# Row maxima and exponentials taken over two PSUM banks at a time

## The reference, cut to what matters

```python
xn = _layernorm(x)
q, k, v = (xn @ Wq, xn @ Wk, xn @ Wv)            # 16, 4 and 4 heads of 16, then rotary angles on q and k
scores = einsum('bshd,bthd->bhst', q, k) / 4
out = einsum('bhst,bthd->bshd', softmax(scores), v) @ Wo
g = silu(ffn(xn))                                 # silu(gate) * up, then down; inner width 1024
x = x + out * g
...                                               # second block: linear attention, 8 routed experts
```

## Time and profile before

| what | us |
|---|---|
| three runs | 353.35, 356.22, 357.67 |
| their median | 356.22 |
| the profiled execution | 353.23 |
| its span, first to last instruction | 351.2 |

### The profile page before, as it was taken

The page is one execution under the profiler, slowest core; times in us unless marked ns, Lnnn a source line. Parts: engine busy times, 40 slices in busy tenths (PEclk is TensorE's granted clock), DMA queues, the critical chain, the costliest instruction groups (busy, mean ns, idle before and its releaser), DMA issues.

```text
span 351.2 us, 4689 instructions
## 1 busy us (share of the span) xinstructions
PE 319.4 (91%) x1598; PEld 188.7 (54%) x1598; DVE 230.7 (66%) x489; ACT 155.8 (44%) x282; POOL 67.4 (19%) x72
## 2 busy tenths in 40 slices
PE   3977799999999999999999999998986999999960
PEld 3655565445555544555554555465654566666640
DVE  3997849767575677877957711289995754456631
ACT  1477414676667455553674564411204222323220
POOL 4008650000020000000000000020673000346641
PEclk9999989999999999999999999998998999999997
DMA  7980000000000000000000040059226990424510
GB/s 245 411 218 2 0 1 2 0 4 0 1 3 2 1 0 3 0 0 4 1 2 1 0 167 15 0 216 367 77 97 189 400 424 32 154 89 136 154 51 11
DMA packets 11370, 30.56 MB, mean 87 GB/s; under 512 B 1773, under 2 KB 8014, under 8 KB 10064
## 3 DMA queue, kind: packets, MB, share of 16 engines
q1 hardware_dynamic: 9392, 26.01, 20.4%
q0 software_dynamic: 1952, 4.22, 3.9%
HBM read 27.22 MB, written 6.60 MB: 96 GB/s over the span
## 4 chain that ended last, share of the span: by engine, by line
PE 74%; DVE 14%; issue 3%; DMA 3%; POOL 2%; ACT 2%; DVEq 0%; POOLq 0%
PE ps L1578 11%; PE ps L1523 9%; PE ps L1491 8%; PE ps L1591 8%; PE ps L1513 7%; PE ps L1646 6%; PE ps L1632 5%; PE ps L1654 5%; PE ps L1428 3%; DVE nmax L1103 3%; PE ps L1453 2%; POOL slot_rows L787 2%; PE ps L1407 2%; PE ps L1622 1%; DMA x<-in_x 1%
## 5 line engine op out<-in xcount | busy, mean ns | idle before, releaser
L1103 DVE TENSOR_REDUCE nmax<-ps 128x1 f32<-128x512 f32 x128 | 85.5, 687 | 34.5 <-PE ps L1491 33.8
L907 ACT ACTIVATE shared<-ps 128x512 f32<-128x512 f32 x128 | 74.2, 594 | 53.8 <-PE ps L1513 52.7
L1491 PE MATMUL ps<-experts 96*128 96x512 bf16 x128 | 48.2, 384 | 1.6 <-DVE experts L1110 1.1
L1513 PE MATMUL ps<-experts 99*128 99x512 bf16 x128 | 48.5, 382 | 0.0
L1591 PE MATMUL ps<-shared,experts 128*128 128x256 f32 x128 | 38.0, 386 | 0.0
L1523 PE MATMUL ps<-shared,experts 128*32 128x512 f32 x256 | 34.1, 605 | 0.3 <-ACT shared L907 0.3
L1491 PEld LDWEIGHTS ps<-experts 96*128 96x128 bf16 x128 | 12.5, 98 | 36.7 <-DVE nmax L1103 18.3
L1591 PEld LDWEIGHTS ps<-shared,experts 128*128 128x128 f32 x128 | 23.3, 191 | 9.8 <-issue 3.4
L777 POOL TENSOR_TENSOR experts<-experts,late_weights 128x768 f32<-128x768 f32 x1 | 1.8, 1805 | 130.8 <-ACT experts L897 130.8
L1428 PE MATMUL ps<-late_weights,xnT 128*128 128x512 f32 (+1 forms) x64 | 23.9, 522 | 0.5 <-DVE shared L1069 0.5
L915 ACT ACTIVATE experts<-ps 96x1024 bf16<-96x1024 bf16 x18 | 17.9, 1018 | 11.6 <-PE ps L1453 11.6
(11 more groups left out here) (209 smaller groups left out, 526.9 us busy)
## 6 DMA issues: line engine op xcount, KB each, us to landing
experts<-in_experts SPq DMA_DIRECT2D x8, 1536.0 KB, 12.6
shared<-in_wgu SPq DMA_DIRECT2D x1, 2048.0 KB, 11.1
slot_rows<-in_empty SPq DMA_DIRECT2D x1, 1950.0 KB, 19.5
late_weights<-slot_rows SPq DMA_DIRECT2D x9, 130.0 KB, 4.2
x<-in_x SPq DMA_DIRECT2D x2, 512.0 KB, 5.5
shared<-in_wdn SPq DMA_DIRECT2D x1, 1024.0 KB, 13.1
token_rows<-x SPq DMA_DIRECT2D x1, 1024.0 KB, 14.4
token_rows<-gx SPq DMA_DIRECT2D x1, 1024.0 KB, 4.9
```

The lines of the kernel that those rows point to most:

```text
L907: nc.scalar.activation(probs[:, n % 2, hh, :], ps[:, 2 + hh % 2, :], ACT.Exp, scale=float(HD) ** -0.5).then_inc(s["exp_done"], 1)
L1103: nc.vector.tensor_reduce(nmax[:, 4 * t + hh:4 * t + hh + 1], ps[:, m % 2, :], AX, ALU.max, negate=True).then_inc(s["max_done"], 1)
L1491: nc.tensor.matmul(ps[:, m % 2, :], qs[0:KS, b, GR * g + hh, P * t:P * t + P], ks[0:KS, b, g, :], start=True, stop=True).then_inc(s["score ...
L1513: nc.tensor.matmul(ps[:, 2 + hh % 2, :], ks[0:KM, b, g, P * t:P * t + P], qs[0:KM, b, GR * g + hh, :], start=True, stop=True).then_inc(s[" ...
```

## The change

A score item becomes a pair of heads: two matmuls into banks 0 and 1, one reduction over both banks that writes two columns of `nmax`. A prob item likewise: two matmuls into banks 2 and 3, one exponential over both. There are then 64 of each where there were 128. Both banks of a pair are read by one instruction, so score pair `m` waits for maximum `m - 1`, and prob pair `q` for exponential `q - 1`. In the loop, a step's first and third place take a prob pair with a score pair right behind it; where a unit's last scores fall due, and in step 0, further score pairs stand at the second (and fourth) place. The values item comes after the score pairs of its place, no longer before them. The planner's assumed durations become 0.44 for a pair on TensorE, 1.1 for an exponential and 1.2 for a maximum. The written-out start keeps its seven transposes and six filling items, now between eight pairs. The count of matmuls stays the same, and every other item is as before.

```diff
-SCORES_OF = ((0, 4), (4, 9), (9, 13), (13, 16))
+SCORES_OF = ((0, 2), (2, 4), (4, 6), (6, 8))
+PAIRS_U = GR * TB // 2
...
-    PE = {"prob": .22, "score": .22, "values": .9, "stack_T": .45, "gate": .65, "up": .65, "down": .43, "heads_norm": .43, "max_rows": .22,
+    PE = {"prob": .44, "score": .44, "values": .9, "stack_T": .45, "gate": .65, "up": .65, "down": .43, "heads_norm": .43, "max_rows": .22,
...
-            self.other("act", .48, ("exp", GR * item[1] + item[2]), t)
+            self.other("act", 1.1, ("exp", 2 * item[1] + item[2]), t)
         elif kind == "score":
-            self.other("dve", .6, ("max", item[1]), t)
+            self.other("dve", 1.2, ("max", item[1]), t)
...
-    for m in range(16):
+    between = ("tt", "t", "te", "tt", "et", "ee", "e", "e")
+    queue = stacks[3:]
+    for m, kinds in enumerate(between):
         plan.append(("score", m))
-        if m in (0, 1, 3, 4, 6, 7, 9):
-            plan.append(stacks[3 + (0, 1, 3, 4, 6, 7, 9).index(m)])
-        elif m in (5, 8, 10, 11, 12, 14):
-            if emit() == ("hidden", 0):
+        for kind in kinds:
+            if kind == "t":
+                plan.append(queue.pop(0))
+            elif emit() == ("hidden", 0):
                 later.append(plan.pop())
...
-            items = [("prob", n, hh)]
+            items = [("prob", n, hh // 2)] if hh % 2 == 0 else []
+            cut = int(bool(scores) and (n == 0 or hh % 2 == 0 or t == TB - 2))
+            items += scores[:cut]
+            scores = scores[cut:]
             if hh == 1 and n > 0:
                 items.append(("values", n - 1))
-            cut = -(-len(scores) // (GR - hh))
-            items += scores[:cut]
-            scores = scores[cut:]
...
-                    nc.scalar.activation(probs[:, n % 2, hh, :], ps[:, 2 + hh % 2, :], ACT.Exp,
+                    nc.scalar.activation(probs[:, n % 2, 2 * hp:2 * hp + 2, :], ps[:, 2:4, :], ACT.Exp,
                                          scale=float(HD) ** -0.5).then_inc(s["exp_done"], 1)
...
-                    nc.vector.tensor_reduce(nmax[:, 4 * t + hh:4 * t + hh + 1], ps[:, m % 2, :], AX, ALU.max,
+                    nc.vector.tensor_reduce(nmax[:, GR * t + 2 * hp:GR * t + 2 * hp + 2].rearrange("p (a o) -> p a o", o=1), ps[:, 0:2, :], AX, ALU.max,
                                             negate=True).then_inc(s["max_done"], 1)
...
-                    if m >= 2:
-                        pe.wait_ge(s["max_done"], m - 1)
-                    nc.tensor.matmul(ps[:, m % 2, :], qs[0:KS, b, GR * g + hh, P * t:P * t + P], ks[0:KS, b, g, :],
-                                     start=True, stop=True).then_inc(s["score_ready"], 1)
+                    if m:
+                        pe.wait_ge(s["max_done"], m)
+                    for a in range(2):
+                        last = nc.tensor.matmul(ps[:, a, :], qs[0:KS, b, GR * g + 2 * hp + a, P * t:P * t + P], ks[0:KS, b, g, :],
+                                                start=True, stop=True)
+                    last.then_inc(s["score_ready"], 1)
...
-                    if q >= 2:
-                        pe.wait_ge(s["exp_done"], q - 1)
-                    nc.tensor.matmul(ps[:, 2 + hh % 2, :], ks[0:KM, b, g, P * t:P * t + P], qs[0:KM, b, GR * g + hh, :],
-                                     start=True, stop=True).then_inc(s["prob_ready"], 1)
+                    if q:
+                        pe.wait_ge(s["exp_done"], q)
+                    for a in range(2):
+                        last = nc.tensor.matmul(ps[:, 2 + a, :], ks[0:KM, b, g, P * t:P * t + P], qs[0:KM, b, GR * g + 2 * hp + a, :],
+                                                start=True, stop=True)
+                    last.then_inc(s["prob_ready"], 1)
```

More of the change, by code:

```diff
@@ L137, in needs @@
         if kind == "prob":
-            _, n, hh = item
-            out = [("exp", GR * n + hh - 2)]
-            return out + [("moved", n // TB)] if hh == 0 and n % TB == 0 else out
+            _, n, hp = item
+            out = [("exp", 2 * n + hp - 1)]
+            return out + [("moved", n // TB)] if hp == 0 and n % TB == 0 else out
         if kind == "score":
-            return [("max", item[1] - 2)]
+            return [("max", item[1] - 1)]
         if kind == "values":
-            return [("exp", GR * item[1] + GR - 1)] + ([("oTs", item[1] // TB - 1)] if item[1] % TB == 0 else [])
+            return [("exp", 2 * item[1] + 1)] + ([("oTs", item[1] // TB - 1)] if item[1] % TB == 0 else [])
         if kind in ("gate", "up", "down"):
@@ L306, in attention_plan @@
         u, t = divmod(n, TB)
-        due_from, due_to = (16 * ((n + 1) // TB + 1) + m for m in SCORES_OF[(n + 1) % TB])
-        scores = [("score", m) for m in range(due_from, due_to) if m < 16 * UNITS]
+        due_from, due_to = (PAIRS_U * ((n + 1) // TB + 1) + m for m in SCORES_OF[(n + 1) % TB])
+        scores = [("score", m) for m in range(due_from, due_to) if m < PAIRS_U * UNITS]
         if n == 0:
-            scores = [("score", 16 + m) for m in range(SCORES_OF[1][1])]
+            scores = [("score", PAIRS_U + m) for m in range(SCORES_OF[1][1])]
         for hh in range(GR):
             pace = start + (total - start) * (GR * n + hh + 1) / (GR * STEPS)
-            items = [("prob", n, hh)]
+            items = [("prob", n, hh // 2)] if hh % 2 == 0 else []
+            cut = int(bool(scores) and (n == 0 or hh % 2 == 0 or t == TB - 2))
+            items += scores[:cut]
+            scores = scores[cut:]
             if hh == 1 and n > 0:
                 items.append(("values", n - 1))
-            cut = -(-len(scores) // (GR - hh))
-            items += scores[:cut]
-            scores = scores[cut:]
             if u + 1 < UNITS and (t, hh) == (TB - 1, 0):
@@ L509, in score_at @@
         def score_at(m):
-            u, r = divmod(m, 16)
+            u, r = divmod(m, PAIRS_U)
             return u // KVH, u % KVH, r // TB, r % TB
@@ L902, in _ @@
                 elif kind == "prob":
-                    _, n, hh = it
-                    act.wait_ge(s["prob_ready"], 4 * n + hh + 1)
-                    if n >= 2 and hh == 0:
+                    _, n, hp = it
+                    act.wait_ge(s["prob_ready"], 2 * n + hp + 1)
+                    if n >= 2 and hp == 0:
                         act.wait_ge(s["values_done"], n - 1)
-                    nc.scalar.activation(probs[:, n % 2, hh, :], ps[:, 2 + hh % 2, :], ACT.Exp,
+                    nc.scalar.activation(probs[:, n % 2, 2 * hp:2 * hp + 2, :], ps[:, 2:4, :], ACT.Exp,
                                          scale=float(HD) ** -0.5).then_inc(s["exp_done"], 1)
@@ L1126, in _ @@
                     u = it[1]
[L1127 removed]
+                    dve.wait_ge(s["max_done"], PAIRS_U * (u + 1))
                     if u:
@@ L1479, in _ @@
                     m = it[1]
-                    b, g, hh, t = score_at(m)
+                    b, g, hp, t = score_at(m)
                     if m == 0:
@@ L1501, in _ @@
                 elif kind == "prob":
-                    _, n, hh = it
+                    _, n, hp = it
                     u, t = divmod(n, TB)
                     b, g = divmod(u, KVH)
-                    if n == 0 and hh < 2:
-                        pe.wait_ge(free_sem[2 + hh], 1)
-                    if t == 0 and hh == 0:
+                    if n == 0 and hp == 0:
+                        for bk in (2, 3):
+                            pe.wait_ge(free_sem[bk], 1)
+                    if t == 0 and hp == 0:
                         pe.wait_ge(row_sem[u % 2], 48 * (u // 2 + 1))
-                    q = GR * n + hh
-                    if q >= 2:
-                        pe.wait_ge(s["exp_done"], q - 1)
-                    nc.tensor.matmul(ps[:, 2 + hh % 2, :], ks[0:KM, b, g, P * t:P * t + P], qs[0:KM, b, GR * g + hh, :],
-                                     start=True, stop=True).then_inc(s["prob_ready"], 1)
+                    q = GR // 2 * n + hp
+                    if q:
[4 more added lines that the diff above has]
+                    last.then_inc(s["prob_ready"], 1)
                 elif kind == "values":
```

17 lines of the change are left out of this document (8 added, 9 removed).

## The result

| | before | after |
|---|---|---|
| median of 15 runs each, us | 354.11 | 358.04 |
| lowest and highest of after | | 355.19, 361.29 |
| profiled execution, its span | 353.23, 351.2 | 358.76, 357.0 |

The ratio of after to before is 1.0101, with a 95% interval of 1.0066 to 1.0135: slower by 1%, 3.6 us (2.3 to 4.8), and within the 2% that count as no change. The forecast was +3.8. Its 360.0 us stood on a median of 356.22 from three runs of before, where the fifteen now have 354.11, so the comparison goes by the difference. Ratios leave disturbed executions out; in one experiment (e9) only three of seven runs were left, and its ratio, 0.9836 (0.9749 to 0.9922), is not used.

What follows compares the result with a forecast made beforehand. The prediction took TensorE's matmuls to bound the loop. Start +2.9, new waits +1.5, old waits -1.0 and end +0.4 summed to +3.8 on a median of 356.2, giving 360.0 us, range 354 to 367.

Steps and rivals of the forecast that it cites:

- Length of the new instructions: Two-bank reductions 1.21 us, exponentials 1.02; relieves VectorE of 10 us and ScalarE of 11, costed at 0.
- Rival D: The two-bank reduction saves nothing (1.37 us), so chains wait oftener; about 363 us, chance 0.05.
- Written-out start: In the start every score pair waits, a chain of 1.89 us setting the pace; +2.9 us (2.5 to 3.6).
- New waits in the loop: In the loop the planner reckons a maximum's chain 0.11 us too short; +1.5 us (0 to 6).
- rival A: Every pair waits, VectorE pieces standing ahead of maxima in list order; median 367 us, chance 0.20.
- Old waits in the loop: Half as many handovers per step recover some of the loop's idle time; -1.0 us (0 to -3).
- the step's tiny idle: Sign against faster loop: real waits of only 0.09 of 5.09 us in the step shown.
- rival B: Nearly all 7 us of idle time between the loop's handovers vanish; median 352.5 us, chance 0.15.
- End: Last prob pair's chain of 1.71 us before its values leaves 0.85 idle; +0.4 us (0 to 0.9).
- the cover: At the end, the last pair's own 0.43 us and about one down block (0.43) lie under its chain.
- Rival C: More idle time in the start brings another half-clock stretch, costing about 1.7 us; median 362, chance 0.10.

Runs made afterwards that it cites:

- e9: Kernel before with prob pairs alone, scores staying single; start 23.84 us, loop 169.21 us.
- e1: Changed kernel with the old start of 16 single scores in two alternating banks; start 22.46 us, ratio to before 1.0044.
- e2: Kernel before with the start in eight score pairs, one reduction over two banks each; start 26.95 us, ratio to before 1.0291.
- e4: Changed kernel with the first unit's reductions reading 256 of 512 columns per bank; start 20.64 us, ratio to before 1.0040.
- e10: Kernel before with score pairs alone, probs staying single; start 25.58 us, loop 171.89 us, ratio to before 1.0124.
- e3: Changed kernel with reductions of all units but the first reading 256 of 512 columns per bank; loop 167.82 us, ratio to before 1.0038.
- e5: Changed kernel with the planner told 1.4 us instead of 1.2 for a pair's maximum; loop 174.59 us, ratio to before 1.0184.
- e12: Kernel before with reductions over 256 of 512 columns in all units but the first; loop 168.94 us, one run.
- e7: Changed kernel with three filling items kept back until the last prob pair is issued; loop 171.10 us, one run.
- e11: e9 with a five-score step's double score moved to its second quarter; loop 168.31 us, median 353.67 us, ratio to before 0.9964.

## Why the prediction was right

The time (+3.8 forecast, +3.6 measured) and the place (the start) were right. That the two numbers agree so closely is partly luck. For the loop with its end the forecast had +0.9 and the milestones have -0.25, so that 2.78 us lie where the forecast looked, and where the rest of the 3.6 lies is not shown. And inside the loop two larger errors cancelled, new waits reckoned too small and recovered idle time reckoned too small.

- *Length of the new instructions.* 1.21 and 1.02 forecast, 1.224 and 1.022 measured. Rival D is out. The relief was 7.2 and 8.8 us, not 10 and 11, since reductions in a train overlap (six in 3.87 us), and so do exponentials, so that 0.687 and 0.594 each overstate the old ones.
- *Written-out start, +2.9.* Measured +3.03 (15.33 - 12.2 = 3.1 to the last maximum, which ends at 46.20 where I had said 45.7; 0.3 of that is a later first score). The chain is 1.92 and not 1.89: the handovers are 0.03 longer. e1, e2, e4 and e10 each confirm it.
- *New waits in the loop, +1.5.* This term was mis-sized: 2.99 us ahead of score pairs (1.7 more than before), as e3 confirms. Two thirds are the bare chain's, as argued. The other third is rival A's mechanism, a VectorE piece ahead of the maximum, at 2 of 56 places; e5 shows what it costs when the plan provokes it. I had it as a case of its own, where it was a part of the forecast.
- *Old waits in the loop, -1.0 (0 to -3).* Also mis-sized: counted as idle time, 1.29 ahead of scores, 0.78 ahead of values and 1.79 at other handovers went, 3.9 in all. I had called the step's tiny idle a sign that little could be won; the waits lay at places outside the one step that I showed. This recovery is rival B's mechanism, and by the count of idle time it kept the loop from growing; e9 shows it for the probs alone, with a loop 2.0 us shorter. How much of it comes from fewer handovers, and how much from VectorE's and ScalarE's relief, which I had put at 0, isn't shown: e12 gives 2.3 us back for some 30 us of VectorE time, but by shortening each reduction, where the change makes each one longer.
- *End, +0.4.* Measured +0.87, near the top of its bounds. Another 0.29 ahead of probs had no term. The step that failed is the cover: no down block was left under the last pair. The chain of 1.72 us (1.71 forecast) was right. e7 shows that moving filling there from the links just before gains nothing; in e9, where two down blocks are there and the link before them doesn't wait, the idle time is 0.41.
- *Rival C.* Both profiles have 3.4 us of half clock behind the start, so it took no part in the difference of 2.78 us at the last values.

The Trainium skill, "Perfetto Trace Analysis", section Optimizing Tensor Performance, Matmuls, advises rotating independent matmul groups through PSUM banks, so that evacuation overlaps the next group's matmuls. The traces agree: without the rotation, score pairs follow each other 1.92 us apart with 3.7 us of TensorE idle in the start.

## What to carry to other kernels

An instruction that covers two banks can save time on its engine (0.15 us of 1.37 here), but if the pair uses up all its banks, every pair becomes a chain of matmul, evacuation and handover. Compare that chain with the distance between pairs, stage by stage: it is free where the distance is longer, and sets the pace where it isn't. The average is not enough: in the step that the prediction counts, pairs lie 2.5 us apart against a chain of 1.92, and yet the bare chain cost 2.0 us in the loop. Where engines walk through one list, work put ahead of a waiting item brings its own pieces on the evacuating engine, and these can delay what the item waits for by more than the work covers (e5). And judge such changes half by half: here one half gains 2.0 us in the loop, and the other loses 3.7 up to the last values.

## What the runs showed of the hardware

The half clock behind the start is not fixed by the order of the work ahead of it. Before, e9 and e11 have the same start up to the first prob, and TensorE waits 2.24, 2.23 and 2.23 us in it for "hidden 0". Behind this wait the granted clock fell to its lower level (1.2 of 2.4 GHz) for 3.4, 6.8 and 0 us, and the start took 22.50, 23.84 and 20.96. The stretches of before, e9 and e11, columns as in the earlier trace rows, the granted clock third from the end:

```profile
45.00:48.00 3.00, 3.00 (x12) 2.21 (x11) 0.81 (x2) 0.59 (x1) 2.92 (x4) 0.61 0.00 1
```

```profile
45.00:48.00 3.00, 3.00 (x10) 1.85 (x10) 0.24 (x1) 0.59 (x1) 2.92 (x3) 0.50 0.00 0
```

```profile
45.00:48.00 3.00, 3.00 (x17) 2.20 (x16) 1.34 (x3) 0.59 (x1) 2.92 (x4) 1.00 0.00 1
```

From this alone a single profile's milestones lie up to 1.5 us above or below those of before, as much as half of the effect studied here. TensorE's busy row, 3.00 of 3.00 in all three, shows nothing of it; the number of matmuls beside it (12, 10, 17) and the clock column do.
